# Order of one step's matmuls in grouped attention: turned scores, maxima's scores and value products

## What is computed

```python
attn = jnp.einsum('bhqd,bhkd->bhqk', q, k) * SCALE
attn = jax.nn.softmax(attn, axis=-1)
x = jnp.einsum('bhqk,bhkd->bhqd', attn, v)
```

## Time and profile before

| | us |
|---|---|
| median of 3 runs | 6562.34 |
| lowest and highest of them | 6562.17, 6564.6 |
| the profiled execution's own time | 6561.7 |
| its span in the trace | 6560.0 |
| PE busy in the span | 4753.5 (72%) |
| DVE busy | 3904.5 (60%) |
| ACT busy | 2772.2 (42%) |
| mean granted clock of PE | 0.841 of full |

### The profile page before, as it was taken

The page is one execution under the profiler, slowest core; times in us unless marked ns, Lnnn a source line. Parts: engine busy times, 40 slices in busy tenths (PEclk is TensorE's granted clock), DMA queues, the critical chain, the costliest instruction groups (busy, mean ns, idle before and its releaser), DMA issues. The chain is left out here.

```text
span 6560.0 us, 102328 instructions
## 1 busy us (share of the span) xinstructions
PE 4753.5 (72%) x24542; PEld 2853.8 (44%) x24542; DVE 3904.5 (60%) x8089; ACT 2772.2 (42%) x5910; POOL 2003.4 (31%) x3012
## 2 busy tenths in 40 slices
PE   7446666491787973897675767597677687995897
PEld 3113333240452331786223645486555563333433
DVE  6335555537547866344477966458866356885564
ACT  2225554115225751322453556435456223771352
POOL 0114443000007630221353554024542114541341
PEclk9558888695898986998777979898889898997897
DMA  4999886100044320210452232102321115332532
GB/s 156 301 319 194 182 185 151 32 0 0 0 154 104 91 69 8 74 40 27 135 148 62 109 110 68 28 13 80 137 75 37 38 35 186 92 76 63 185 114 89
DMA packets 368620, 650.62 MB, mean 99 GB/s; under 512 B 66474, under 2 KB 179019, under 8 KB 368160
## 3 DMA queue, kind: packets, MB, share of 16 engines
q1 hardware_dynamic: 296744, 453.06, 22.5%
q0 software_dynamic: 71488, 193.32, 12.1%
HBM read 373.08 MB, written 237.78 MB: 93 GB/s over the span
## 5 line engine op out<-in xcount | busy, mean ns | idle before, releaser
L1115 DVE TENSOR_REDUCE t_nmax<-t_aps 128x2 f32<-128x1024 f32 x700 | 837.6, 1222 | 287.2 <-PE t_aps L1037 281.8
L1222 ACT ACTIVATE t_expT<-t_bps 128x512 f32<-128x512 f32 x1290 | 701.2, 599 | 293.2 <-PE t_bps L1056 243.4
L1056 PE MATMUL t_bps<-t_Q,t_K 51*128 51x512 f32 (+2 forms) x1290 | 530.8, 473 | 59.3 <-ACT t_expT L1222 43.2
L1037 PE MATMUL t_aps<-t_K,t_Q 49*128 49x512 f32 (+2 forms) x1400 | 469.3, 464 | 64.3 <-DMA t_K<-k_halves 29.2
L1056 PEld LDWEIGHTS t_bps<-t_Q,t_K 51*128 51x128 f32 (+2 forms) x1290 | 231.3, 191 | 531.4 <-ACT t_expT L1222 373.4
L2413 DVE TENSOR_TENSOR f_hl<-f_h,f_hh 128x512 fp32r<-128x512 f32 x192 | 204.3, 1064 | 423.1 <-ACT f_hh L2344 423.1
L1083 PE MATMUL t_ops<-t_expT,t_V 128*17 128x512 f32 (+1 forms) x2560 | 419.9, 624 | 0.4 <-ACT t_expT L1222 0.4
L3823 ACT ACTIVATE t_relsb<-t_relsb,t_nmax 128x128 f32<-128x128 f32 (+3 forms) x515 | 279.3, 559 | 313.4 <-DVE t_nmax L3796 309.8
L3757 PE MATMUL t_tps<-ident,t_relsb 128*128 128x128 f32 x1280 | 255.5, 306 | 182.5 <-ACT t_expT L3642 173.5
L2703 POOL TENSOR_TENSOR a_crossed<-a_qsb,a_tab 128x256 f32<-128x256 f32 x272 | 267.4, 1005 | 299.9 <-ACT a_qsb L2650 267.5
L1156 POOL DMA_DIRECT2D t_Q<-q_halves x525 | 272.0, 520 | 140.8 <-POOLq L78 73.3
(11 more groups left out here) (418 smaller groups left out, 12262.5 us busy)
## 6 DMA issues: line engine op xcount, KB each, us to landing
rel<-r_out SPq DMA_DIRECT2D x128, 640.0 KB, 5.4
t_relsb<-rel SPq DMA_DIRECT2D x128, 256.0 KB, 4.3
t_Q<-q_halves POOLq DMA_DIRECT2D x420, 64.0 KB, 2.6
t_K<-k_halves POOLq DMA_DIRECT2D x420, 64.0 KB, 2.6
t_relsb<-rel SPq DMA_DIRECT2D x128, 192.0 KB, 3.6
k_halves<-a_parts SPq DMA_DIRECT2D x48, 512.0 KB
q_halves<-a_parts SPq DMA_DIRECT2D x48, 512.0 KB, 5.5
t_relsb<-rel SPq DMA_DIRECT2D x128, 128.0 KB, 3.5
```

Of the source, the lines that this page charges most:

```text
L1037: last = nc.tensor.matmul(aps[:, (t * PPG + i) % 2, x, :], operand(Qr, KA, p, h, slice(t * P, (t + 1) * P)), operand(Kr, KA, p, h, slice(0 ...
L1056: nc.tensor.matmul(bps[:, slot_of(kb, j), :], operand(Kr, KB, p, h, slice(kb * P, (kb + 1) * P)), operand(Qr, KB, p, h, slice(0, S)), star ...
L1115: nc.vector.tensor_reduce(nmax[:, g, t, i * HPT:(i + 1) * HPT], aps[:, (t * PPG + i) % 2], AX.X, ALU.max, negate=True).then_inc(s["maxed"], 1)
L1222: nc.scalar.activation(expT[:, kb % RING, j, :], bps[:, slot_of(kb, j), :], ACT.Exp).then_inc(s["expo"], 1 + (PAD if end else 0))
```

## The change

The hand-written order of the step on PE is replaced by a loop over the pairs. In the four-head stages the order was T0' T1' S0 T2' PV T3' S1 and becomes T0' T1' S0 PV T2' T3' S1. In the two-head stage, where PPG is 1, it was T0' PV T1' S0 and becomes PV T0' T1' S0. No instruction is added or removed, and no wait's count is changed.

```diff
-                    for j in range(HG - 1):
-                        turned(p1, G1, g1, kb1, j)
-                        if j == 1:
-                            scores(p2, G0 + DEPTH, g2, kb, 0)
-                    products()
-                    turned(p1, G1, g1, kb1, HG - 1)
-                    scores(p2, G0 + DEPTH, g2, kb, PPG - 1)
+                    for i in range(PPG):
+                        if i == PPG - 1:
+                            products()
+                        for x in range(HPT):
+                            turned(p1, G1, g1, kb1, i * HPT + x)
+                        scores(p2, G0 + DEPTH, g2, kb, i)
```

## The result

The changed kernel takes 6677.69 us (median of 4 runs, 6660.59 to 6685.66) against 6563.47 us of the kernel before in the same comparison. The ratio is 1.0179 with a 95% interval from 1.0154 to 1.0203: it is slower by 101 to 133 us. The forecast was 6662 in a range from 6615 to 6700.

The account below looks back on a forecast made before the run. A loop between ACT and PE was taken to set the regular step, with both waiting on each other's results. 6561.7 + 53 (two-head stage) + 47 (four-head stages) = 6662 us, range 6615 to 6700.

Parts of the forecast that it names:

- t1 and t3: The two four-head stages: 64 groups at +0.74 us each were forecast to lose 47 us together.
- t7: The two-head stage: steps of 2.65 us against 2.17 (2.43 with the shift), 32 groups, +53 us (to +61).
- The loop through T1' and the bank of E2': Four-head stages: T1' of the next step waits until E2' has read its bank; steps 2.82 and 3.31 us.
- The passage of 0.66: Four-head stages, PE from T1' to PV without T2' between: 0.34 + 0.32 = 0.66 us, other end 0.77.
- The choice of 0.32 over 0.43: Four-head stages, S0o to PV: 0.32 taken because S0o doesn't wait for a semaphore; 0.77 as passage would add 28 us.
- start-up and passes that ACT begins late: Rest of t1 and t3 outside 64 groups (737 of 774 us); ACT 2.16 us idle at passes, untouched by the change.
- E0' can't run beside PV: Two-head stage: T0' queues behind PV and ACT waits for it; 0.53 from T0' to E0', regular step +0.48 us.
- The shift's step: Two-head stage, step with the shift: 2.65 us against 2.43, +0.22; up to 2.9 if small products still held PV.
- DVE, POOL, SP and the DMAs at nothing: Other engines cost nothing: DVE gets further from being the bound, the others work two and three groups ahead.
- Rival 1: Only the two-head stage loses, the four-head passage T1' to PV hides or the shift's gain pays; 6618 us, chance 0.15.
- Rival 2: Four-head stages: PE is the bound and pairing saves a slot, groups fall to 10.19 us; total 6530, chance 0.05.
- Rival 3: Two-head stage: PE's new idles bring its clock down to 1.2 GHz, +82 us on top, 6744; chance 0.06.

## Why the prediction was right

- **Sign and size.** Forecast +100 us, measured +114 (101 to 133). By stage: t1 and t3 +47 forecast, +47.4 in the profiles; t7 +53 forecast, +70.2. That the first pair agrees to 0.4 us is partly chance: the groups give 64 x 0.76 = 49, and what lies outside them moved by some 10 us between executions with PE's clock, which is more than the difference. The total stayed in the range although t7 was off by 17 us, because the range had 38 us above its sum, kept for other terms.
- **Four-head stages.** The loop through T1' and the bank of E2' is as forecast: steps of 2.82 and 3.31 us, groups of 12.28 against 12.26. The passage of 0.66, put together from two places of the trace before (0.34 and 0.32), is what the trace after shows. The choice of 0.32 over 0.43 had a reason that a later run bears out: in the order with T1' directly ahead of PV, where the matmul before PV is one that waits, the passage is 0.43. The run with S0 ahead of T1' shows that this passage, and not the amount of matmuls, was what cost: 0.8 us of a group went with it. The 37 us of t1 and t3 outside the groups were put down to start-up and passes that ACT begins late; most of that time is PE's clock below full there, which the prediction didn't say, but the sum didn't use it.
- **Two-head stage.** The mechanism (E0' can't run beside PV) was right, and one term was mis-sized: from T0' to E0' are 0.66 and not 0.53 us. The 0.53 was read at an exponential that has one wait. E0' has a second wait and an empty instruction behind it, which had been covered in the kernel before. With these put ahead of the wait the step is the forecast's 2.65. 4 x 32 x 0.13 = 17 us is the whole difference of this stage. The shift's step was forecast at 2.65 to 2.9 and came out like the other three, at 2.78, so the small products don't hold PV there.
- **DVE, POOL, SP and the DMAs at nothing.** Right: DVE's idle grew by 100 us, and none of the chains named them.
- **Rival 1** (only the two-head stage loses) fell with the run of the four-head stages alone, 1.0049 with its interval above 1, and groups of 12.29 us. **Rival 2** (PE's own matmuls are the bound, so that pairing wins) fell with the same run; PE did pair T2' with T3' and S1e with S1o, and the groups grew all the same. **Rival 3** (the clock) didn't happen: 0.96, 0.95 and 0.99, with an idle of 0.6 us ahead of PV in a step of t7 (0.48 was estimated). Whole stages at the lower clock do occur in this program, with halved products, but with idles of PE below 0.3 us in the new order, so those runs don't show that gaps between matmuls bring it about.

## What to carry to other kernels

When an engine's hand-written order is changed, the sum is made over the loop from one engine's result back to itself, and the question for each moved instruction is which results of the other engine could be worked on during the long operation, and now can't. An instruction that waits makes everything queued behind it wait: put work that is free to go in front of it. A step that is read from one instruction isn't valid for its neighbour with more waits: count the instructions between the arrival and the start.

## What the runs showed of the hardware that was not expected

- Less work made the program slower. With half the value products in the four-head stages, PE's granted clock stayed at 0.50 (1.2 GHz of 2.4) for 497 us in the one order and 467 us in the other, where it is 0.95 to 0.98 with the full products and 0.99 with twice as many. Both stages were entered at a granted clock of 0.50 in all these kernels; with the halved products it didn't rise. The cost was 15.43 us a group where 10.6 were expected. In the two-head stage half the products left it at 0.98 in the new order and 0.94 in the old. So how near a stage stands to such a fall can't be read off from its clock.
- A wait and an empty instruction on ACT, between the semaphore's arrival and the exponential, cost 0.13 us together in the open (0.66 against 0.53 us from T0' to E0') and nothing where the score is there early (groups of 11.52 and 8.93 us with either order of the waits).
- PE's clock in stretches that no kernel changed settled differently from execution to execution, and one stretch took 254, 272 or 282 us by it. Within the four-head stages a group that begins a pass took 13.35 us at 1.00 and 17.21 at 0.66. That is more than the effect of some of the edits, so small effects had to be read from the loops.
